# Attention and mixture-of-experts block on one core: gates applied to the experts' inner units, W2 as the weight in two column halves, 64-row float32 pairs, centred W_v and W_dec

## The reference, cut to what matters

```python
x = L0_attn_x                                  # (4, 512, 128) float32
x = x + ln(attn(ln(x)))                        # ln without gain and shift
x = x + ln(ffn(ln(x)))
# attn: softmax((h@Wq+bq) (h@Wk+bk)^T / sqrt(128)) @ (h@Wv+bv)
# ffn:
spikes = sigmoid(h @ W_enc + b_enc)            # 128 -> 256
cont   = spikes @ W_s2c + b_s2c                # 256 -> 64
probs  = softmax(cont @ Wr + br)               # 8 experts, the two best kept, renormalised: gate
hid    = relu(cont @ W1[e] + b1[e])            # 64 -> 128, for all 8 experts
y      = hid @ W2[e] + b2[e]                   # 128 -> 64
moe    = sum_e gate[e] * y[e]
dec    = sigmoid(moe @ W_c2s + b_c2s) @ W_dec + b_dec   # 64 -> 256 -> 128
return ln(dec) * ln_g + ln_b
```

## Time and profile before

| | |
|---|---|
| device time, median of 3 runs | 161.86 us (161.65 to 161.9) |
| profiled execution, first to last instruction | 160.3 us |
| busy: PE | 138.7 us (87%), 820 records |
| busy: PEld | 104.4 us (65%) |
| busy: DVE | 130.0 us (81%), 504 instructions |
| busy: ACT | 66.8 us (42%), 128 instructions |
| busy: POOL | 29.9 us (19%) |
| DMA | 4.16 MB, mean 26 GB/s |

### The profile page before, as it was taken

One profiled execution on the slowest core, in us unless ns is written; L12 is line 12 of the kernel. 1 busy time (PEld: TensorE's weight loads), 2 busy tenths in 40 slices (PEclk: granted clock), 3 DMA queues, 4 the chain that ended last, 5 costly groups with the idle time before them and its releaser, 6 DMA issues.

```text
span 160.3 us, 2496 instructions
## 1 busy us (share of the span) xinstructions
PE 138.7 (87%) x820; PEld 104.4 (65%) x828; DVE 130.0 (81%) x504; ACT 66.8 (42%) x128; POOL 29.9 (19%) x55
## 2 busy tenths in 40 slices
PE   7697999589999989999999799999998889994810
PEld 2254686356589775768897757687994477983700
DVE  1686379999979996699999962897999759979883
ACT  3114662182961317467811246397203566003200
POOL 1452243102013100122211100204310002200131
PEclk9999999999999999999999999999999999999555
DMA  3499300000000000000010000000000010000101
GB/s 97 114 203 222 105 4 2 0 0 0 0 4 0 0 2 0 2 4 0 0 65 4 2 0 0 0 0 4 0 0 0 2 70 0 0 0 0 65 0 65
DMA packets 5597, 4.16 MB, mean 26 GB/s; under 512 B 1987, under 2 KB 4562, under 8 KB 5586
## 3 DMA queue, kind: packets, MB, share of 16 engines
q1 hardware_dynamic: 5586, 4.02, 9.3%
HBM read 2.97 MB, written 1.05 MB: 25 GB/s over the span
## 4 chain that ended last, share of the span: by engine, by line
DVE 55%; PE 23%; issue 9%; POOL 3%; SPq 2%; DMA 2%; ACT 2%; POOLq 1%; DVEq 0%
DVE stats L887 10%; DVE gated L1012 6%; DVE mean_var L890 4%; DVE moe L1022 4%; PE ps_f L718 4%; POOL rstd L352 3%; DVE neg_max L928 3%; DVE attn L903 3%; PE ps_f L638 3%; DVE hn L903 3%; PE ps_f L630 2%; PE ps_s L586 2%; DMA x_in<-in_L_attn_x 2%; DVE x_mid L945 2%; DVE z L1061 2%
## 5 line engine op out<-in xcount | busy, mean ns | idle before, releaser
L352 POOL TENSOR_TENSOR rstd<-var_eps,minus_half 128x2 f32<-128x2 f32 (+1 forms) x32 | 26.1, 815 | 122.9 <-DVE var_eps L896 104.1
L688 PEld LDWEIGHTS ps_f<-w,hidden 128*128 128x128 f32 x256 | 31.0, 192 | 1.8 <-issue 1.3
L688 PE MATMUL ps_f<-w,hidden 128*128 128x64 f32 x256 | 30.3, 272 | 0.5
L443 ACT ACTIVATE hidden<-ps_f,bias_cols 128x512 f32<-128x512 f32 x28 | 18.0, 689 | 9.2 <-PE ps_f L669 9.2
L1022 DVE TENSOR_REDUCE moe<-gated 128x64 f32<-128x512 f32 x16 | 16.6, 1035 | 0.1
L586 PE MATMUL ps_s<-kT,qT 128*128 128x512 f32 x32 | 16.3, 602 | 0.2 <-DVE kT L1092 0.2
L404 ACT ACTIVATE probs<-ps_s,neg_max 128x512 f32<-128x512 f32 x16 | 11.0, 685 | 8.3 <-DVE neg_max L928 8.3
L668 PE MATMUL ps_f<-cont_parts,w_hi 128*128 128x512 f32 x28 | 13.8, 493 | 0.3 <-DVE products L962 0.3
L928 DVE TENSOR_REDUCE neg_max<-ps_s 128x1 f32<-128x512 f32 x16 | 10.8, 685 | 2.9 <-PE ps_s L586 2.8
L409 ACT ACTIVATE probsT<-ps_t 128x512 f32<-128x512 f32 x16 | 9.6, 598 | 7.0 <-PE ps_t L596 7.0
L669 PE MATMUL ps_f<-cont_parts,w_lo 128*128 128x512 f32 x28 | 11.1, 395 | 0.0
(11 more groups left out here) (188 smaller groups left out, 250.8 us busy)
## 6 DMA issues: line engine op xcount, KB each, us to landing
x_in<-in_L_attn_x SPq DMA_DIRECT2D x4, 256.0 KB, 3.8
out<-x_out SPq DMA_DIRECT2D x3, 256.0 KB, 2.0
w_raw<-in_L_ffn_W SPq DMA_DIRECT2D x2, 256.0 KB, 4.5
b_all<-in_L_ffn_b SPq DMA_DIRECT2D x1, 256.0 KB, 4.6
w<-in_L_ffn_W SPq DMA_DIRECT2D x1, 256.0 KB, 5.5
out<-x_out SPq DMA_DIRECT2D x2, 128.0 KB, 1.7
w_enc<-in_L_ffn_W_enc SPq DMA_DIRECT2D x1, 128.0 KB, 4.4
w_dec_raw<-in_L_ffn_W_dec SPq DMA_DIRECT2D x1, 128.0 KB
```

What stands on the lines that cost most here:

```text
L352: nc.gpsimd.tensor_tensor(rstd[part], var_eps[part], minus_half[:, t0:t1], ALU.pow).then_inc(g_rstd[n], 1)
L443: nc.scalar.activation(hidden[:, e], hidden_bank(b, e)[:, :], ACT.Relu, bias=bias_cols[:, R_B1 + e:R_B1 + e + 1]).then_inc(a_h, 1)
L688: mm = nc.tensor.matmul(y[:, e * M:(e + 1) * M], hidden[:, e, t * P:(t + 1) * P], w2[:, e], start=False, stop=(e == E - 1))
```

## The change

It replaces the expert part's arithmetic, and the schedule of all engines is written anew around it.

1. Gates. `turn_gates` turns `gate` on PE (4 turns), ACT copies the 8 rows out (`gate_out`), SP writes them to a DRAM buffer, waits, and reads them back to all 128 partitions with four loads of 512 KB (`gate_all`, 2 MB a batch).
2. Inner units. `hidden_pair`: an expert's inner units are one float32 product over 64 rows; the two experts of a pair use the upper and the lower 64 rows (`cont` holds the same cont in both), into two banks. There is no split of W1 and cont. DVE evicts each with `gate_hidden`: max(product, -b1) times gate, 128x512, from PSUM. ACT has no ReLU to do.
3. Outputs. `expert_out(b, e)`: W2[e] (128 rows, 64 columns) is the weight, the gated inner units move, 256 tokens at a time, into the upper 64 partitions of `ps_t` for the first half and the lower 64 for the second, and the eight experts sum in PSUM. The biases come first as one product with (b1[e] W2[e] + b2[e]) as weights and the turned gates moving. The DVE's multiply, sum and copy and PE's turn of moe are gone.
4. `to_spikes` and `route` use 64-row float32 products too.
5. W_v, b_v, W_dec and b_dec have their row means taken off, so attention output and decoded tokens have mean zero. Their statistics become sums of squares on ACT (`attn_squares`, `dec_square`, 128-column Square with accumulation), and `mid_stats` makes x_mid in one DVE operation instead of two.
6. Start. W_v and b_v are loaded by ACT's queue; DVE centres them. PE's product of ones with W_dec waits for the centred W_dec.

The diff, cut to its core:

```diff
@@ PE
-                    pe.wait_ge(d_qkv, 64)
+                    pe.wait_ge(d_qk, 32)
...
+            def turn_gates(b):
+                pe.wait_ge(v_gate, 9 * (b + 1))
+                for t in range(T):
+                    mm = nc.tensor.transpose(ps_c[0:E, 1, t * P:(t + 1) * P], gate[:, b % 2, t], ident[:, :])
+                mm.then_inc(pe_gT, 1)
+            def hidden_pair(b, p):
...
+                for i in range(2):
+                    e = 2 * p + i
+                    if p >= 2:
+                        pe.wait_ge(v_gated, E * b + e - 3)
+                    half = slice(i * M, (i + 1) * M)
+                    nc.tensor.matmul(hidden_bank(e), w1[half, e], cont[half, b % 2],
+                                     start=True, stop=True).then_inc(pe_h, 1)
+            def expert_out(b, e):
+                pe.wait_ge(v_gated, E * b + e + 1)
+                for h in range(2):
+                    mm = nc.tensor.matmul(ps_t[h * M:(h + 1) * M, 0:SH], w2[:, e], gated[:, e, h * SH:(h + 1) * SH],
+                                          start=False, stop=(e == E - 1))
...
-            pe.wait_ge(g_dec, 1)
+            pe.wait_ge(v_wdec, 9)
             for c in range(HC):
...
             for b in range(B):
...
+                if b >= 1:
+                    if more:
+                        turn_probs(n, 0)
+                        scores(n, 2)
+                    pe.wait_ge(a_c2s, HC * b)
+                    decode(b - 1, 0)
+                    decode(b - 1, 1)
+                    if more:
+                        attend(n, 0)
+                        turn_probs(n, 1)
+                        scores(n, 3)
+                    decode(b - 1, 2)
+                    decode(b - 1, 3)
+                    if more:
+                        attend(n, 1)
+                        turn_probs(n, 2)
+                    if more2:
+                        turn_x(m)
+                    turn_gates(b)
+                    if more:
+                        attend(n, 2)
+                        turn_probs(n, 3)
+                    if more2:
+                        project_q(m)
+                    if more:
+                        attend(n, 3)
+                    if more2:
+                        project_k(m)
+                hidden_pair(b, 0)
+                hidden_pair(b, 1)
+                if more2:
+                    project_v(m)
+                expert_biases(b)
+                expert_out(b, 0)
+                expert_out(b, 1)
+                hidden_pair(b, 2)
+                expert_out(b, 2)
+                expert_out(b, 3)
+                hidden_pair(b, 3)
+                if more:
+                    turn_h(n)
+                expert_out(b, 4)
+                expert_out(b, 5)
+                if more:
+                    encode(n, 0)
+                    encode(n, 1)
+                expert_out(b, 6)
+                expert_out(b, 7)
+                if more2:
+                    scores(m, 0)
+                    scores(m, 1)
+                if more:
+                    to_cont(n)
+                to_spikes(b)
+                if more:
+                    route(n)
@@ SP, in the loop over b
+                sp.wait_ge(a_gT, b + 1)
+                sp.dma_start(gates_dram[b].ap(), gateT[0:E, b % 2]).then_inc(d_gate_out, 16)
+                sp.wait_ge(d_gate_out, 16 * (b + 1))
...
+                for j in range(4):
+                    two = slice(2 * j, 2 * j + 2)
+                    sp.dma_start(gate_all[:, b % 2, two],
+                                 gates_dram[b].ap()[two].partition_broadcast(P)).then_inc(d_gate_in[b % 2][j], 16)
@@ ACT, in the loop, b >= 1
+                    if more:
+                        exps(n, 0)
+                    for c in range(HC):
+                        spike2(b - 1, c)
+                    if more:
+                        exps(n, 1)
+                        pT_out(n, 0)
+                    second_exp(b)
+                    if more:
+                        exps(n, 2)
+                        pT_out(n, 1)
+                        exps(n, 3)
+                    dec_square(b - 1, 0)
+                    if more:
+                        pT_out(n, 2)
+                        attn_squares(n, 0)
+                    gate_out(b)
@@ DVE
+            def gate_hidden(b, e):
+                dve.wait_ge(pe_h, E * b + e + 1)
+                dve.wait_ge(d_gate_in[b % 2][e // 2], 16 * (b // 2 + 1))
+                if e == 0 and b >= 1:
+                    dve.wait_ge(pe_moe, b)
+                nc.vector.scalar_tensor_tensor(gated[:, e], hidden_bank(e), b1_minus[:, e:e + 1],
+                                               gate_all[:, b % 2, e], ALU.max, ALU.mult).then_inc(v_gated, 1)
...
             nc.vector.memset(zeros[:, :], 0.0).then_inc(v_zeros, 1)
+            dve.wait_ge(d_v, 32)
+            for i in range(2):
+                nc.vector.bn_stats(wv_stats[:, i], wv_raw[:, i]).then_inc(v_wv, 1)
...
             x_stats(0)
             x_norm(0)
```

More of the change, by code:

```diff
@@ L44, in attention_moe_block @@
     out_dram = out.rearrange("b (p t) d -> b p t d", t=T)
+    gates_dram = [nc.dram_tensor(f"gates{b}", [E, S], F32) for b in range(B)]
     with ExitStack() as ctx:
@@ new lines, in spike2_last, with dec_square @@
+            def spike2_last(h, c):
+                b = B - 1
+                act.wait_ge(pe_c2s, b + 1)
+                nc.scalar.activation(spikes2[:, b % 2, c, h * SH:(h + 1) * SH], ps_c[:, h, c * SH:(c + 1) * SH],
+                                     ACT.Tanh, bias=bias_half[:, HC + c:HC + c + 1], scale=0.5).then_inc(a_c2s, 1)
+            def dec_square(b, i):
+                if b == B - 1:
+                    act.wait_ge(pe_dec, parts_done(LN_DEC, b, i))
+                else:
+                    act.wait_ge(v_z1, parts_done(LN_DEC, b, i))
+                for t in range(*parts(LN_DEC, b)[i]):
+                    nc.scalar.activation(dec_squares[:, b % 2, t], decoded(b, t), ACT.Square,
+                                         accum_out=dec_square_sum[:, b % 2, t:t + 1]).then_inc(a_dec_square, 1)
@@ new lines, in decode @@
+            def decode(b, t):
+                if b == 0 and t == 0:
+                    pe.wait_ge(v_bdec, 7)
+                nc.tensor.matmul(decoded(b, t), ones_bf[:, :], b_dec_stack[:, :], start=True, stop=False)
+                for c in range(HC):
+                    mm = nc.tensor.matmul(decoded(b, t), spikes2[:, b % 2, c, t * P:(t + 1) * P], w_dec[:, c],
+                                          start=False, stop=(c == HC - 1))
+                if any(t == t1 - 1 for _, t1 in parts(LN_DEC, b)):
+                    mm.then_inc(pe_dec, 1)
@@ L1215, in _ @@
+                for e in range(4, E):
+                    gate_hidden(b, e)
+                if b >= 1:
+                    z_norm(b - 1, 0)
+                if more2:
+                    row_max(m, 0)
+                    row_max(m, 1)
+                if b >= 1:
                     z_add(b - 1, 0)
```

916 lines of the change are left out of this document (367 added, 549 removed).

## The result

The changed kernel takes 174.53 us (median of 4 runs, 173.86 to 175.63); the kernel before took 161.88 on the same chip (161.65 to 163.11). The ratio is 1.0759 with a 95% interval of 1.0701 to 1.0817. The profiled span is 171.7 us, against 160.3 before. The forecast of 168 had the sign right and half of the size: +12.65 us came where it had +6.1. In what follows the medians are over all runs of a kernel, and the ratios leave out a run that lies over 1.5% above the fastest of the same kernel.

The account below looks back on a forecast made before the run. PE was taken to bound a full iteration, DVE close behind. Stage changes of 4.0 + 0.3 - 1.1 + 1.0 + 1.8 = +6.0 on 160.3 gave a span of 166.3, with 1.6 around it 168 us; range 157 to 179.

Parts of the forecast that it names:

- the price of the first part: Start to route(0): 44.4 us for 40.4, +4.0, from later loads, ACT Squares and PE's wait for the centred W_dec.
- the last batch: Batch 3 to the end: 32.7 us for 30.9, +1.8, including +1.5 for low clock after PE's rest.
- the overlap of pairs: Products on two array halves: only half records overlap, so a lone pair costs three half-products, k in a row k + 1.
- side by side: Rival for PE's pairs: both products take the time of one; 159.5 us, chance 0.19.
- the forecast's own sign of being wrong: On PE: the prediction is wrong if the array's halves overlap fully.
- its other sign: Batches 1 and 2: prediction wrong if both stages shrink below 28 us, the ACT and DMA chain being shorter than walked.
- The array's cut: PE switching between whole array, rows and columns about ten times an iteration: 0.09 us each, 0.9 us in all.
- drain: Rival on PE: each change of the array's cut costs 0.2 us or more, +1.3 to +2 a batch; 174 us, chance 0.14.
- The middle stages: Batches 1 and 2: 32.0 us for 33.1, -1.1, and 29.6 for 28.6, +1.0.
- the chain of the gates: ACT's copy, write, load, DVE at 15.3 us: as long in batch 2 as in batch 1; stage +1.0.
- Batch 0: Stage behind route(0): 27.6 us for 27.3, +0.3; PE stands 1.5 us before the first gates.
- The walk: One iteration followed from the end of route(b) in each engine's written order: 32.0 us; for the last batch 29.1 at full clock.

Follow-up runs that it names:

- e5: Changed kernel with both experts of a pair on the same 64 rows: 183.72 us, ratio 1.1287.
- e7: Changed kernel without W2's column halves, all 512 tokens moving once into the upper 64 partitions: 188.67 us, ratio 1.158.
- e2: Changed kernel with the centring of W_dec and b_dec on DVE ahead of batch 0's row_max(0, 3): 169.94 us, ratio 1.0358.
- e6: Changed kernel with e1 and e2 together, 14 filler products, and the last batch's gates copied ahead of the decoded tiles' squares on ACT: 164.04 us, ratio 1.0105.
- e11: e8 with 17 instead of 13 warm-up products on PE: 162.32 us, ratio 1.0005.
- e4: Changed kernel without the gates' read-back from DRAM; gate_hidden multiplies with a constant 0.125 filled by POOL: 170.85 us, ratio 1.0497.
- e1: Changed kernel with DVE's wait for W_v and b_v and their statistics behind x's first normalisation: 172.87 us, ratio 1.0636.
- e3: Changed kernel with 16 products of zeros on PE before the last batch's first W2 product: 172.69 us, ratio 1.0619.
- e8: e6 with batch 0's gates made, turned and copied out earlier, ahead of batch 2's x work: 162.93 us, ratio 1.0028.

## Why the prediction was right in its sign and half in its size

Two steps of the forecast carry the miss: the price of the first part (+7.0 for +4.0), where it let 2.3 us of PE's late start come back and put nothing down for the clock, and the last batch (+4.4 for +1.8). They are taken up below in their order. The step on which its rivals turned, the overlap of pairs, was wrong too, but in the other direction: the forecast priced the pairs about 1.0 us too dear in batch 1. With the right price it would have stood further from the measured time, so part of its nearness is luck.

**A pair of half-array products: wrong step.** The forecast let a pair cost three half-products (1.29 us alone, 2.15 for a run of two pairs, 1.07 for four W2 products). Measured: 1.06 alone, 1.91 for the run, 1.02 for the four, and e5 and e7 show 1.81 to 1.91 where nothing can overlap. The rival "side by side" was right on this, and so the forecast's own sign of being wrong, that the halves overlap fully, came true all but 0.1 to 0.2 us a group; its other sign, middle stages under 28 us, did not. The Trainium skill (TensorEngine Tiling (Array Packing), Key Properties) says that different tiles execute in parallel; the 1.91 against 3.63 us agree, for float32 products of two records each.

**The array's cut: right.** The forecast took 0.9 us an iteration. The pair alone at 1.06 against 0.86 for one product of this length, and encode's two whole-array products at 1.91 between W2's groups (99.07 to 100.98) against 2 x 0.86, show 0.1 to 0.2 at each change. Summed over batch 1: the removed work was 13.0 us, the new one takes 10.1 by starts (inner units 4.0, W2 4.25, biases 0.48, to_spikes 0.96, gates 0.44). That is 2.9 less, and the stage gave 2.1. PE is idle for about 1 us of this stage in both kernels, so the 0.8 between went to other products, by the starts just read to the neighbours of the changes. The same page of the Trainium skill has a change of mode drain the engine; the starts just read show 0.1 to 0.2 us a change, as the forecast had it. The rival "drain" at 174 us, which came nearest to the time, put the loss into every batch; the runs show most of it around PE's waits, so its nearness is chance.

**The middle stages: right in kind.** -2.1 and +0.7 for -1.1 and +1.0. In batch 1 the difference of 1.0 is the pairs. In batch 1 `gate_hidden` 0 waits for PE's own inner units, not for the gates, and W2 starts 16.3 us behind the route (forecast 17.0); the gates left ACT 9.3 us behind it (forecast 10.2). Batch 2's +0.7 is not sure: with the same code and the full clock in this stage, e2, e6 and e11 have 28.8, 28.6 and 28.8, at most 0.2 above before. The forecast held the chain of the gates for the bound there; e4 gives it 1.0 against the changed kernel but only 0.3 to 0.5 against these.

**The first part, +7.0 for +4.0: the term that failed most.** The forecast had PE's product with W_dec 5.2 us later than before, 1.1 more for the b1 x W2 products, and 2.3 of this coming back. Measured, the product starts 6.1 later (33.12 for 26.99), the b1 x W2 products take 1.8, and only 0.9 comes back. The first 0.9 of the miss is ahead of the wait: the start's shift of 1.6 us reached the first scores as 2.9 (forecast 1.1), since products between 10 and 13.6 us ran at the lower clock. The wait itself was foreseen well (3.6 us until 32.2; 3.06 until 33.12). The next 0.7 is the half clock on the b1 x W2 products (1.8 for 1.0 in e2). The last 1.4 is the return that failed to come, and this is not the clock's alone: in e2, with the full clock from the product with W_dec to the route, the product is 2.85 later than before, the b1 x W2 products take 1.0, the part ends 3.2 later, and so 0.6 comes back where the forecast had 2.3. With both causes removed (e6) the first part is 41.9, still 1.5 above before. The b1 x W2 products cost PE 1.0 by their starts; whether the rest is ACT's squares or the new order no run shows.

**Batch 0, +1.4 for +0.3.** PE's wait before the first gated units was put at 1.5 us and was 2.32. The trip of the gates is the reason (e4): the write leaves at 53.90 and the first gated units start at 59.69, 5.8 us, where the forecast had 4.8 from the end of ACT's copy (10.2 to 15). The write was quicker than said (1.5 to the loads' issue, forecast 2.1), the first load slower (4.3 from its issue to its first use, forecast 2.7). The stage's mean clock is 0.94; with the full clock (e1, e3) the stage is 28.0 and 28.1, so 0.6 to 0.7 of the 1.4 is the clock. In e8 the write leaves 4.2 us behind the route instead of 6.4 in e6, but the loads follow it after 2.7 us instead of 1.5 (why, no run shows), and the first gated units start 1.4 us earlier.

**The last batch, +4.4 for +1.8: right mechanism, mis-sized.** The walk had the biases done at 7.9 and the first gated units at 11.6 us behind the route; they came at 7.5 (143.28 + 0.65 - 136.4) and 11.4 (147.82). So the place was right. The low clock costs 2.2 (e3). The forecast put it at 3.4 and let the wait for loads cover half, 1.5 left; the cover was smaller. The other 1.9 us lie behind the first gated units: with the clock held up (e3) some 21.8 us pass from there to the end, where the walk had 19.6. The trace shows one stretch that grew. These are the last decoded tiles on PE, in the kernel before (at half clock) and in the changed one:

```profile
151.60 1.17 PE L745 MATMUL ps_f<-w_dec,spikes 128*128 128x128 f32 x4
```

```profile
161.61 0.66 PE L726 MATMUL ps_a<-w_dec,spikes 128*128 128x128 f32 x4
```

From their end to the end of the span it is 7.5 us before and 9.4 now. Before, the two halves of the last batch were decoded 3.3 us apart (147.19 and 150.53), and DVE worked on one while PE made the other. Now the experts' sum is complete for all tokens at once, the halves are decoded 1.1 us apart (159.94 and 161.05), and DVE has nearly all of both still ahead of it. The walk gives no figure for this stretch, and no run separates it, so how much of the 1.9 it is stays open. The trip itself is worth 2.8 here (e4), the copy ahead of the squares and the fillers together 3.5 (e6).

**Bandwidth: right that it doesn't matter.** The slices reach 347 GB/s, more than the 222 that the estimate used, and batch 1 runs the same with and without the loads.

## What to carry to other kernels

Products on different halves of the array, in rows or in columns, are worth their full factor of two even in float32, less 0.1 to 0.2 us for each group; count them so when PE bounds the stage. But a new wait of PE for work that another engine has queued late costs its length and then the low clock behind it. Such a clock can take back in one execution what was gained ahead of the wait (e1's profile) and not in others (e1's median), so compare the medians before a stage of one profile is read as the effect of an edit. Before moving a step forward on an engine, look at what it waits for there and what it pushes back; in a stage that PE bounds, 1.2 us of ACT's idling in front of the early copy lengthened the stage by 1.6.

## What the runs showed of the hardware

The overlap of float32 halves (0.96 us a pair against 1.81 on the same rows; 1.02 against 1.86 for two experts on column halves). The granted clock behind a rest: after 4.7 us without work the next two groups took twice their time (1.91 for 1.02, 2.01 for 1.06), and after 3.1 us without work the b1 x W2 products did (1.8 for 1.0). 16 products with zeros in the rest lifted the stage's mean clock from 0.84 to 0.93, and PE still waited 1.07 us behind them (e3); with 14 it was 0.93 in e6 and 0.90 in e11. Four loads of 512 KB issued within 1.75 us reach 321 to 347 GB/s in a slice of 4.3 us, and the first of them is used 4.2 to 4.3 us after its issue. A Square of 128 columns with its accumulator read takes ACT 0.25 us in a row (the forecast had 0.35).
